# GpSimd takes part of the weight splitting in the first tiles, and the last tile orders its products differently

## The reference

```python
x = x + xattn(layernorm(x), ctx_512, W_k, b_k, gamma, beta)
n = layernorm(x)
scores = einsum('btd,ed->bte', n, Wg)
topk_s, topk_i = top_k(scores, 2)
w = softmax(topk_s), spread over the 8 experts
for e in range(8):
    h = silu(n @ W1[e].T) * (n @ W2[e].T)
    y = y + w[..., e:e + 1] * (h @ W3[e].T)
x = x + y
```

## Time and profile before

| | before |
|---|---|
| median of three runs | 374.2 us |
| the profiled execution's own time | 373.96 us |
| its span | 371.8 us |
| TensorE busy | 351.3 us (94%) |
| VectorE busy | 250.3 us (67%) |
| ScalarE busy | 264.4 us (71%) |
| GpSimd busy | 175.5 us (47%) |
| first up product of tile 0 starts | 111.26 us |
| down product of tile 0 starts | 121.41 us |
| down product of tile 6 starts | 162.66 us |
| last down product starts | 361.10 us |

### The profile page before, as it was taken

The page is one execution under the profiler, slowest core; times in us unless marked ns, Lnnn a source line. Parts: engine busy times, 40 slices in busy tenths (PEclk is TensorE's granted clock), DMA queues, the critical chain, the costliest instruction groups (busy, mean ns, idle before and its releaser), DMA issues.

```text
span 371.8 us, 8177 instructions
## 1 busy us (share of the span) xinstructions
PE 351.3 (94%) x2284; PEld 230.1 (62%) x2284; DVE 250.3 (67%) x554; ACT 264.4 (71%) x451; POOL 175.5 (47%) x243
## 2 busy tenths in 40 slices
PE   8999999998989999999999999999999999999980
PEld 7555676777656555566666666666666666666640
DVE  2367688978979999976565666656565747475740
ACT  2478999995999899957575757566666666666640
POOL 2134846778631546544444435363535454545331
PEclk9999999999669999999999999999999999999997
DMA  6999999999730344445454545445454545453524
GB/s 217 416 412 409 333 417 416 357 341 396 236 89 0 59 86 63 82 87 91 81 89 85 85 89 84 89 74 100 70 104 66 104 69 107 63 99 70 87 32 53
DMA packets 21944, 57.70 MB, mean 155 GB/s; under 512 B 4816, under 2 KB 4944, under 8 KB 20368
## 3 DMA queue, kind: packets, MB, share of 16 engines
q0 software_dynamic: 8736, 20.61, 32.0%
q1 hardware_dynamic: 12016, 30.30, 21.5%
q10 hardware_dynamic: 1152, 6.29, 4.6%
HBM read 38.25 MB, written 18.94 MB: 154 GB/s over the span
## 4 chain that ended last, share of the span: by engine, by line
PE 76%; DVE 5%; DMA 5%; issue 4%; ACT 4%; POOL 3%; POOLq 1%; SPq 1%; ACTq 0%; DVEq 0%
PE bank L1297 37%; PE bank L1333 20%; PE bank L1288 4%; DMA Wp<-in_w 3%; PE bank L1317 3%; PE bank L1154 3%; PE bank L1085 2%; PE bank L1200 1%; DMA out<-kvj_s,sidx 1%; PE bank L1174 1%; PE bank L1127 1%; ACT Wp L646 1%; DVE Wp L870 1%; PE bank L1183 1%; POOL rstd L439 1%
## 5 line engine op out<-in xcount | busy, mean ns | idle before, releaser
L1032 DVE SCALAR_TENSOR_TENSOR stage<-W,w3sc,stage 128x512 f16<-128x512 f16 x117 | 84.2, 748 | 6.1 <-ACT stage L698 6.1
L1333 PE MATMUL bank<-stage,n_s 128*128 128x512 f16 (+1 forms) x351 | 82.2, 379 | 4.7 <-issue 3.3
L698 ACT ACTIVATE stage<-W,w3sc 128x512 f16 x117 | 80.1, 718 | 0.0
L1297 PE MATMUL bank<-Wp,kvg_s 128*128 x480 | 78.2, 312 | 0.9 <-DVE kvg_s L1038 0.9
L1297 PE MATMUL bank<-Wp,kv_s 128*128 x456 | 74.3, 312 | 0.4 <-DVE kv_s L1038 0.4
L1048 DVE TENSOR_TENSOR n_s<-bank,n_s 128x384 f16<-128x384 f32 x39 | 21.7, 557 | 68.2 <-ACT n_s L713 68.2
L1297 PEld LDWEIGHTS bank<-Wp,kvg_s 128*128 128x128 f16 x480 | 46.7, 98 | 26.7 <-issue 1.8
L1297 PEld LDWEIGHTS bank<-Wp,kv_s 128*128 128x128 f16 x456 | 44.3, 98 | 25.4 <-issue 2.1
L539 POOL DMA_INDIRECT out<-oT_s,sidx x20 | 32.1, 1606 | 57.0 <-ACT oT_s L729 53.4
L518 POOL DMA_INDIRECT ng_s<-n_table,gidx x39 | 43.2, 1108 | 32.1 <-POOL wm L532 22.7
L1333 PEld LDWEIGHTS bank<-stage,n_s 128*128 128x128 f16 (+1 forms) x351 | 33.8, 97 | 38.9 <-issue 6.1
(11 more groups left out here) (198 smaller groups left out, 529.4 us busy)
## 6 DMA issues: line engine op xcount, KB each, us to landing
Wp<-in_w SPq DMA_DIRECT2D x8, 1408.0 KB, 10.3
W<-in_w ACTq DMA_DIRECT2D x8, 768.0 KB, 7.3
stage<-in_xT SPq DMA_DIRECT2D x4, 1024.0 KB, 8.9
W<-in_x SPq DMA_DIRECT2D x12, 256.0 KB, 9.7
out<-W SPq DMA_DIRECT2D x12, 256.0 KB, 8.8
n_table<-n_s SPq DMA_DIRECT2D x8, 256.0 KB, 7.8
n_table<-x_s SPq DMA_DIRECT2D x8, 256.0 KB, 7.7
stage<-in_x SPq DMA_DIRECT2D x4, 256.0 KB, 8.7
```

Of the source, the lines that this page charges most:

```text
L698: eng.activation(w3p[t % 2][:, c * D:(c + 1) * D], W3[:, bass.ds(e * W3N + c * D, D)], ACT.Copy, scale=w3sc[:, bass.ds(e, 1)]).then_inc(s_ ...
L1032: eng.scalar_tensor_tensor(w3p[r][:, W3N + c * D:W3N + (c + 1) * D], W3[:, bass.ds(e * W3N + c * D, D)], w3sc[:, bass.ds(e, 1)], w3p[r][:, ...
L1297: mm = eng.matmul(bank[2 * which + r][:, 0:H], n_, w_, start=(c == 0 and k == 0), stop=(c == DC - 1 and k == 2))
L1333: mm = eng.matmul(ybank(t - 1)[:, :], h_, w_, start=(c == 0 and k == 0), stop=(c == HC - 1 and k == 2))
```

## The change

Two parts are made at once.

**First tiles.** GpSimd makes the second half (h = 1) of the up weights of experts 2, 4 and 6 in three instructions of 128 x 1408 each: `scale_half` (f32 in place), `high_half` (a cast to f16) and `low_half` (f32 minus f16). For expert 1 it makes the high part of the second half alone (`scaled_high`). ScalarE loses four `w12_high`, VectorE three `w12_low`. A new semaphore `s_pw` counts GpSimd's ten pieces, and `low_ready` waits for whichever engine made a half. `w12_high(1, 0)` moves ahead of `mT_evac(0)` on ScalarE, and `w3_square(3)` behind it. On VectorE `w12_low(1, *)` moves ahead of `w3_sums` and `w3_scale`. The eight semaphores of the W3 loads become four.

**Last tile.** With `t = 38` (`NT - 1`) TensorE turns the hidden rows of tile 37 first, then does the first up product, the down product of tile 37, the second up product, 4 filler products, the turn of tile 38's hidden rows, 3 filler products, and the down product of tile 38 with all high·high and high·low products ahead of the low·high ones. Only these last wait for the hidden rows' low part. ScalarE takes the high part of tile 37's hidden rows ahead of the SiLU of tile 38, VectorE all three `w3_low` ahead of the hidden rows.

```diff
+POOL_LOW = (2, 4, 6)
+POOL_HIGH = (1,) + POOL_LOW
+POOL_PIECES = (("high", 1), ("scale", 2), ("high", 2), ("low", 2), ("scale", 4), ("high", 4), ("low", 4), ("scale", 6), ("high", 6), ("low", 6))
+WARM_HIDDEN = 4
+WARM_SPLIT = 3
...
+            def scaled_high(k):
+                raw, high, low = second_half(k)
+                eng.wait_ge(s_wsc, 1)
+                low_ready(eng, k - 1, 0)
+                eng.tensor_scalar(high, raw, wscale[:, k:k + 1], None, ALU.mult).then_inc(s_pw, 1)
+            def scale_half(k):
+                raw, high, low = second_half(k)
+                eng.wait_ge(s_wsc, 1)
+                eng.tensor_scalar(raw, raw, wscale[:, k:k + 1], None, ALU.mult).then_inc(s_pw, 1)
+            def high_half(k):
+                raw, high, low = second_half(k)
+                low_ready(eng, k - 1, 0)
+                eng.wait_ge(s_pw, pool_count("scale", k))
+                eng.tensor_copy(high, raw).then_inc(s_pw, 1)
+            def low_half(k):
+                raw, high, low = second_half(k)
+                low_ready(eng, k - 1, 1)
+                eng.wait_ge(s_pw, pool_count("high", k))
+                eng.tensor_tensor(low, raw, high, ALU.subtract).then_inc(s_pw, 1)
...
             gather(2)
+            scaled_high(1)
+            scale_half(2)
+            high_half(2)
+            low_half(2)
...
             for t in range(NT):
                 row_weights(t)
                 gather(t + 3)
+                if t == 0:
+                    scale_half(4)
+                if t == 1:
+                    high_half(4)
+                if t == 2:
+                    low_half(4)
+                if t == 3:
+                    scale_half(6)
+                    high_half(6)
+                if t == 4:
+                    low_half(6)
...
             w3_square(2)
-            w3_square(3)
+            w12_high(1, 0)
...
             mT_evac(0)
-            w12_high(1, 0)
-            w12_high(1, 1)
+            w3_square(3)
...
             low_rows(0)
+            w12_low(1, 0)
+            w12_low(1, 1)
             w3_sums()
             w3_scale()
-            w12_low(1, 0)
-            w12_low(1, 1)
...
+            def last_tiles():
+                t = NT - 1
+                e = eng.value_load(ecoli[0:1, t:t + 1], min_val=0, max_val=E - 1)
+                turn_hidden(t - 1)
+                first_up(t, e)
+                down(t - 1)
+                second_up(t, e)
+                warm(oh[:, :, :, :].rearrange("p g k e -> p (g k e)"), WARM_HIDDEN, 1)
+                turn_hidden(t)
+                warm(oh[:, :, :, :].rearrange("p g k e -> p (g k e)"), WARM_SPLIT, 1)
+                last_down(t)
```

More of the change, by code:

```diff
@@ L244, in build @@
         s_w = [sem(f"s_wl{i}") for i in range(E)]
-        s_w3 = [sem(f"s_w3_{i}") for i in range(E)]
+        s_w3 = [sem(f"s_w3_{i}") for i in range(PAIRS)]
+        s_pw = sem("s_pw")
         s_wq, s_wqp, s_wsum, s_wmax, s_wsh, s_wrs, s_wsc, s_wrec, s_winv = [
@@ L317, in ring_free, with high_count, low_count, pool_count @@
                 eng.wait_ge(s_S, G)
+        def high_count(k, h):
+            return 2 * k + h + 1 - sum(j < k or (j == k and h == 1) for j in POOL_HIGH)
+        def low_count(k, h):
+            return 2 * k + h + 1 - sum(j < k or (j == k and h == 1) for j in POOL_LOW)
+        def pool_count(piece, k):
+            return POOL_PIECES.index((piece, k)) + 1
+        def low_ready(eng, k, h):
+            if h == 1 and k in POOL_LOW:
+                eng.wait_ge(s_pw, pool_count("low", k))
+            else:
+                eng.wait_ge(s_lo, low_count(k, h))
         def ybank(t):
@@ L709, in tile @@
                     eng.activation(act_a[r], bank[r][:, 0:H], ACT.Silu, scale=winv[:, bass.ds(e, 1)]).then_inc(s_a, 1)
[L710 to L713, removed]
+                if t > 0 and t != NT - 1:
+                    hidden_high(t - 1)
                 if t == 0:
@@ L861, in w12_low @@
             def w12_low(k, h):
-                if k >= E:
+                if k >= E or h == 1 and k in POOL_LOW:
                     return
-                eng.wait_ge(s_hi, 2 * k + h + 1)
-                wait(eng, s_lo, 2 * k)
+                if h == 1 and k in POOL_HIGH:
+                    eng.wait_ge(s_pw, pool_count("high", k))
+                else:
+                    eng.wait_ge(s_hi, high_count(k, h))
+                if k > 0:
+                    low_ready(eng, k - 1, 1)
                 cols = slice(h * WH, (h + 1) * WH)
@@ new lines, in down_part, with down @@
+            def down_part(t, k, j, first, last):
+                for c, (h0, n) in enumerate(HCH):
+                    h_ = hT[t % 2][0:n, k, c * P:(c + 1) * P]
+                    w_ = w3p[t % 2][0:n, j * W3N + c * D:j * W3N + (c + 1) * D]
+                    mm = eng.matmul(ybank(t)[:, :], h_, w_, start=first and c == 0, stop=last and c == HC - 1)
+                return mm
+            def down(t):
+                eng.wait_ge(s_w3l, HC * (t + 1))
+                eng.wait_ge(s_hl, t + 1)
+                wait(eng, s_y, t - 1)
+                for c, (h0, n) in enumerate(HCH):
+                    h_high, h_low = [hT[t % 2][0:n, k, c * P:(c + 1) * P] for k in range(2)]
+                    w_high, w_low = [w3p[t % 2][0:n, k * W3N + c * D:k * W3N + (c + 1) * D] for k in range(2)]
+                    for k, (h_, w_) in enumerate(((h_high, w_high), (h_low, w_high), (h_high, w_low))):
+                        mm = eng.matmul(ybank(t)[:, :], h_, w_, start=(c == 0 and k == 0),
+                                        stop=(c == HC - 1 and k == 2))
+                mm.then_inc(s_yp, 1)
```

90 lines of the change are left out of this document (54 added, 36 removed).

## The result

The changed kernel takes 392.9 us, median of five runs (392.0 to 394.9), against 374.3 us for the kernel before (373.6 to 376.8). The ratio is 1.050, with a 95% interval of 1.047 to 1.053. The prediction was 384.6 us with a range up to 389.5: the sign is right, and the time lies above the range, with a loss of 18.5 us where 10.6 was forecast. The profiled execution took 394.93 us, the longest of the five.

A forecast was written before the change was run, and what follows sets the result against it. VectorE was taken to bound the first six tiles, TensorE the thirty after. 4.3 at the start plus 6.5 in the six tiles minus 0.2 at the end, 10.6 on 373.96, gave 384.6 us, range 380 to 389.5.

The forecast's parts named there:

- What bounds the kernel: Tile stage: VectorE bounds the first six tiles, 6.88 us each; TensorE bounds the thirty after, 6.28 us each.
- The mechanism: First tiles: GpSimd and two-SBUF-operand VectorE instructions wait for each other's whole instruction, 10.5 us of VectorE waits in tiles 1 to 6.
- the scaling at 1.8 us: GpSimd's scaling of 1408 columns, priced from a 512-column tensor_scalar of 0.77 us; upper end 2.1 us.
- the six tiles: Tiles 1 to 6: 10.5 us of waits against 4.8 us taken off VectorE, a loss of 6.5 us taken.
- the walk: Step through GpSimd's and VectorE's instructions with assumed durations and mutual waiting; 8 us with all low prices, 16 with high.
- The late square: Start: the last W3 square moved back delays TensorE's small product and tile 1, 1.6 us, bounds 1.2 and 2.2.
- The clock's fall: Rival, 12%: TensorE's clock falls in new holes before tiles 0 and 4; one half-rate tile, 6 us more, 390.6 us.
- W3's small tensor_scalars: Start, VectorE: no wait counted for them; W3's scale and low_rows(1) were to end at 117.3.
- the 4.3 forecast: Start: down product of tile 0 at 125.7 instead of 121.41, 4.3 us late, with the late square's 1.6 inside.
- Gathers and scatters as free: GpSimd: gathers and scatters move behind the pieces at no cost while the delay is under a tile, 6.3 us.
- The last tile: End: the new order wins 0.2 us, bounds 0.0 and 0.4, as the last scatter waits for the one before.
- the scatters' spacing of 5.45: End: the last two scatters stand 5.45 us apart, the second waiting only for the first's landing.

The follow-up runs named there:

- Experiments 3 and 4: The changed kernel with GpSimd's pieces replaced by memsets, which read nothing: one per piece, 378.33 us (1.011); several, about as long as the pieces, 379.33 us (1.014).
- experiment 10: The changed kernel with its four GpSimd scalings given a second factor of 1.0: 384.89 us, ratio 1.028 to the kernel before.
- experiments 6 and 7: 6: only the changed order at the start, GpSimd's lists empty, 378.65 us; 7: the same with 28 filler products instead of 10, 376.02 us.
- experiment 8: The changed kernel with only GpSimd's four pieces ahead of the tiles (experts 1 and 2), both new orders kept: 382.35 us, ratio 1.022.

## Why the prediction was wrong in size and right in kind

- **What bounds the kernel: right.** Six first tiles bound by VectorE and the rest by TensorE; the thirty later ones did not move (188.69 against 188.70 us).
- **The mechanism: right.** VectorE stands still for a whole GpSimd piece and the other way round. Experiments 3 and 4 show it by its absence, and only the pieces' length was changed in experiment 10.
- **The step that failed: the scaling at 1.8 us** ("in proportion to 512 columns it would be 3.5 and 2.1, the upper ends"). It takes 3.87, and 3.84 alone. The row that priced it is a tensor_scalar with two operations and this one has one; the prediction took the operation's name for its form. The form of four instructions is worth 8.0 us of the time (experiment 10: 392.9 to 384.9). In the six tiles VectorE's waits come to some 12.8 us with the long scaling and 9.3 with the short one, where the walk had 10.5. The clock is part of it: its mean there is 0.97 with the long scaling and 1.00 with the short one.
- **The range.** The walk's 8 and 16 us on 373.96 give 382 to 390, not the stated 380 to 389.5. Neither reaches 392.9.
- **The late square: 1.6 us forecast, 4.6 measured alone**, 1.9 of it the square and 2.6 what the filler won back, 1.4 of that seen as clock in the profiles (experiments 6 and 7). The clock's fall was given as a rival with one tile at half rate, 6 us, while it happened beside the forecast's mechanism, behind several holes of some 3 us, after each of which the up products took some 1.5 us more.
- **W3's small tensor_scalars: taken as free, not free.** They wait up to 2.6 us, and W3's scale and `low_rows(1)` stand behind them; the prediction had those done at 117.3, and in experiment 10, where the scaling is cheap, `low_rows(1)` ran from 121.49 (2.7 us of that is the late token table). What these waits alone cost the kernel was not tried.
- **Sum by places.** In experiment 10 the down product of tile 0 is 7.0 us later, 2.7 of it ahead of the tile stage, so 4.4 against the 4.3 forecast; the six tiles take 46.23 - 41.09 = 5.1 more against 6.5. Some of the agreement of 384.9 with 384.6 is therefore luck: the scaling is cheaper there (1.44) than the 1.8 assumed, the small tensor_scalars and the clock at the start were left out, and these roughly cancel.
- **Gathers and scatters as free: right**, TensorE waits for none of them in the tile stage. **The last tile: right in kind**, 0.2 us forecast and 0.45 measured; the scatters' spacing of 5.45, held fixed in the forecast, was 5.1 to 5.4.
- **Open:** the 2.0 us by which the token table was late in the profile after. The clock fell at about 92 us there and at about 95 before, ahead of all that the change touches but the W3 semaphores, and with these experiment 8 has the product at 103.61. In the profiles of the experiments this product starts 0.0 to 2.7 us later than in before's, so it varies between executions; what sets it was not tried.

## What to carry to other kernels

Before work is given to GpSimd, price each instruction in its exact form, with the same number of operations, at the same size; and when the trace has only a cousin, let the range reach as far as the form is unknown. Then count every VectorE instruction that reads two SBUF operands, or is a small tensor_scalar between SBUF tiles, as standing still for the whole of a GpSimd piece: moving 1.6 us of VectorE work onto a GpSimd chain of 6 to 8 us lost in every variant tried here, as VectorE was the bound there. A new hole ahead of TensorE cost more than the delay itself, by 1.4 us in the profile and 2.6 in the medians of experiments 6 and 7, and filler products in the hole brought that part back.

## What the runs showed of the hardware that was not expected

- A GpSimd tensor_scalar of 1408 columns takes 3.84 us with one operation and 1.44 us with a second, idle one (times 1.0).
- VectorE's two-input instructions keep their 1.68 us beside a GpSimd memset; a VectorE tensor_scalar of 8 columns does not, and takes 1.3 us instead of 0.17.
- An idle stretch of TensorE of 2.65 us was followed, once work had resumed, by about 3 us at a granted clock near 0.5 (0.53 for 115 to 118 us in experiment 6; 1.00 for the same stretch with the hole filled).
